# Attention on one core: probabilities and values turned by DMA as two planes of 16-bit halves instead of by TensorE

## What is computed

```python
y = einsum('bct,bcd->bdt', x, cond_weights[itok])          # (64, 64, 1024)
qkv = y @ attn_qkvw + attn_qkvb                            # 32 heads of 32, q, k and v
scores = einsum('bhqd,bhkd->bhqk', q, k) * 32 ** -0.5
probs = softmax(scores)
ctx = einsum('bhqk,bhkd->bhqd', probs, v)                  # 64 x 64 scores per sequence and head
x = x + ctx @ attn_ow + attn_ob                            # output stage
x = x + ffn(expert_lora(x))                                # expert and feed-forward stage
```

## Time and profile before

| | |
|---|---|
| median of 3 runs | 2267.62 us (2263.91 to 2267.73) |
| the profiled execution's own time | 2266.86 us |
| its span, first to last instruction | 2265.2 us |
| mean granted TensorE clock, share of full | 0.986 |
| busy: TensorE matmuls, weight loads | 2172.2 us, 1772.7 us |
| busy: VectorE, ScalarE, GpSimd | 1441.5 us, 732.3 us, 1385.6 us |

### The profile page before, as it was taken

How to read it: one execution, slowest core, us unless ns; L and a number is a source line. 1 busy time by engine, 2 the same in 40 slices (tenths; PEclk the granted TensorE clock), 3 DMA queues, 4 the chain that set the end, 5 groups by cost and what they waited for, 6 DMA issues and landing times.

```text
span 2265.2 us, 46621 instructions
## 1 busy us (share of the span) xinstructions
PE 2172.2 (96%) x18848; PEld 1772.7 (78%) x18848; DVE 1441.5 (64%) x2392; ACT 732.3 (32%) x1182; POOL 1385.6 (61%) x1135
## 2 busy tenths in 40 slices
PE   6999999999999999999999899999899999999996
PEld 5888887888877888878888678888777778777774
DVE  5344564455464454655554776566688888888986
ACT  4222242222242222332222422222344344444342
POOL 6888778877778887797776740000355555555553
PEclk9999999999999999999999999999999999999998
DMA  4112122212132112212112543557644434444432
GB/s 146 56 62 65 63 85 75 72 53 66 58 101 73 58 57 66 84 49 70 53 65 73 200 159 125 191 172 207 157 103 106 107 94 101 111 111 104 108 85 83
DMA packets 220828, 219.35 MB, mean 97 GB/s; under 512 B 83570, under 2 KB 152306, under 8 KB 220146
## 3 DMA queue, kind: packets, MB, share of 16 engines
q1 hardware_dynamic: 217794, 213.65, 31.6%
q0 software_dynamic: 2864, 3.28, 0.9%
HBM read 152.92 MB, written 50.33 MB: 90 GB/s over the span
## 4 chain that ended last, share of the span: by engine, by line
PE 83%; DVE 7%; issue 2%; POOL 2%; SPq 2%; ACT 2%; DMA 1%; POOLq 0%; DVEq 0%; ACTq 0%
PE acc L699 33%; PE acc L1543 15%; PE acc L1095 6%; PE att L1095 6%; PE att L1568 5%; PE att L730 3%; PE att L1517 3%; PE acc L1576 2%; PE att L739 2%; PE att L754 2%; DVE prob L539 2%; PE acc L1550 2%; DVE total L535 1%; PE acc L713 1%; SPq L265 1%
## 5 line engine op out<-in xcount | busy, mean ns | idle before, releaser
L699 PE MATMUL acc<-y_hi,w_slot_hi 128*128 128x512 f32 x1344 | 541.5, 403 | 26.1 <-DVE unit L556 7.5
L699 PE MATMUL acc<-y_hi,w_slot_lo 128*128 128x512 f32 x1344 | 527.1, 392 | 0.0
L699 PE MATMUL acc<-y_lo,w_slot_hi 128*128 128x512 f32 x1344 | 526.9, 392 | 0.0
L345 POOL TENSOR_TENSOR w_slot_lo<-w_raw,w_slot_hi 128x512 fp32r<-128x512 f32 x329 | 423.2, 1286 | 26.3
L699 PEld LDWEIGHTS acc<-y_hi,w_slot_hi 128*128 128x128 f32 x1344 | 254.4, 189 | 86.2 <-issue 30.3
L343 POOL CAST w_slot_hi<-w_raw 128x512 fp32r<-128x512 f32 x329 | 218.8, 665 | 155.8 <-PE acc L699 130.7
L699 PEld LDWEIGHTS acc<-y_hi,w_slot_lo 128*128 128x128 f32 x1344 | 254.3, 189 | 54.6
L699 PEld LDWEIGHTS acc<-y_lo,w_slot_hi 128*128 128x128 f32 x1344 | 254.9, 190 | 48.3
L348 POOL TENSOR_TENSOR w_raw<-w_raw 128x512 f32<-128x512 f32 x188 | 258.5, 1375 | 30.0 <-DMA w_raw<-wu 25.6
L546 DVE COPY cx<-att 128x512 f32<-128x512 f32 x63 | 43.5, 691 | 305.9 <-PE att L754 276.8
L556 DVE TENSOR_TENSOR unit<-acc,unit 128x512 f32<-128x512 f32 x144 | 98.6, 687 | 172.9 <-PE acc L699 168.3
(11 more groups left out here) (175 smaller groups left out, 3940.4 us busy)
## 6 DMA issues: line engine op xcount, KB each, us to landing
w_raw<-wu SPq DMA_DIRECT2D x192, 256.0 KB, 3.1
f_x_all<-x_T SPq DMA_DIRECT2D x64, 512.0 KB, 5.5
c_raw<-context_T SPq DMA_DIRECT2D x16, 1024.0 KB, 6.2
out<-f_raw SPq DMA_DIRECT2D x32, 512.0 KB, 3.4
context_T<-cx SPq DMA_DIRECT2D x63, 256.0 KB, 3.5
x_raw<-x SPq DMA_DIRECT2D x27, 512.0 KB, 4.5
xa<-xT SPq DMA_DIRECT2D x12, 1024.0 KB, 7.4
x_T<-xa SPq DMA_DIRECT2D x48, 256.0 KB, 2.0
```

What stands on the lines that cost most here:

```text
L345: pool.tensor_tensor(w_lo[:, k], raw, w_hi[:, k].bitcast(F32), ALU.subtract).then_inc(w_set, 1)
L699: ins = pe.matmul(bank, w[:, k, c, :], v[:, k, c, :], start=(k in (0, 1, 5) and c == 0 and i == 0), stop=(c == C // 2 - 1 and i == 2), ski ...
```

## The change

The transposes leave TensorE. ScalarE parts each fp32 word of a 128x512 plane into its upper and lower 16 bits (`words`, a copy of 1024 16-bit elements into `pw` or `vw`), issues a DMA transpose of the 128x1024 16-bit elements from its own queue (into `pv` or `vv`), and after landing joins the halves again into `prob_T` or `v_s` (another copy of 1024 elements). There are 61 x 2 such trips for the probabilities and 64 for the values; the last three iterations keep TensorE's turn (`TURNED`). Three ScalarE operations (two copies and a DMA issue) stand where one copy out of PSUM stood.

Places: scores now stand at 0, 5, 10 and 15, and in the same place TensorE mixes the iteration before. The other engines follow `behind`: VectorE normalises plane 0 one slot and plane 1 two slots behind the scores, ScalarE sends plane 0 out two slots and plane 1 three slots behind, and joins both four slots behind. Values go out at 0, 7, 10 and 15 and come back at 3, 9, 13 and 18 (in the last duo: out at 0, 2, 4, 6).

The four new tiles lie where `x_raw` lies. So a block's first three x tiles are loaded only in slots 4 and 5 of the unit before, when the trips of that place are done, and the trips that come next wait until the y products have read the tiles (`x_done`). The staging of y uses `uo[0]` from the second block on.

```diff
+    vw, vv, pw, pv = (nc.alloc_sbuf_tensor_at(n, shape, U16, offset=X_AT + 4096 + at) for n, shape, at in (
+        ("vw", [P, 2, HALF], 0), ("vv", [P, 2 * HALF // P, P], 2048),
+        ("pw", [P, 2, 2, HALF], 4096), ("pv", [P, 2, 2 * HALF // P, P], 8192)))
...
+    PLACES = (0, 5, 10, 15)
+
     def scored(U, k):
 
         duo, at = place(U, k)
-        return 4 * duo + (0, 4, 10, 15).index(at) if at in (0, 4, 10, 15) else None
-
-    def turned(U, k):
+        return 4 * duo + PLACES.index(at) if at in PLACES else None
+
...
+    def behind(U, k, steps):
+
+        q = SLOTS * U + k - steps
+        return scored(*divmod(q, SLOTS)) if q >= 0 else None
+
+    def values_out(U, k):
         duo, at = place(U, k)
-        return 4 * duo + (3, 9, 14, 19).index(at) if at in (3, 9, 14, 19) else None
-
-    def mixed(U, k):
-
+        steps = (0, 2, 4, 6) if duo == DUOS - 1 else (0, 7, 10, 15)
+        return 4 * duo + steps.index(at) if at in steps else None
+
+    def values_back(U, k):
         duo, at = place(U, k)
-        if at == 0:
...
-        return 4 * duo + (4, 10, 15).index(at) if at in (4, 10, 15) else None
-
-    def values(U, k):
-
-        duo, at = place(U, k)
-        return duo, {0: (0, 1), 3: (2, 3)}.get(at, ())
+        steps = (2, 4, 6) if duo == DUOS - 1 else (3, 9, 13, 18)
+        return 4 * duo + steps.index(at) if at in steps else None
+
+    def words(ap):
+
+        return ap.bitcast(U16).rearrange("p (n h) -> p h n", h=2)
+
+    TURNED = ITERS - 3
...
+    def stage(r):
+
+        return uo[0] if r else uo[1]
...
+            last = 16 * r - 4
+            if r and t >= 3:
                 sp.wait_ge(y_mm, i - 2)
-            elif i >= PAIRS:
-                sp.wait_ge(y_mm, i - PAIRS + 1)
-            arrived = x0_in[i // 2 - 1] if 3 <= i < PAIRS else x_in[(i - PAIRS) % 3 if i >= PAIRS else i]
+            elif r:
...
+                sp.wait_ge(y_mm, PAIRS * r)
+                if t == 0:
+                    sp.wait_ge(v_set, last + 1)
+                elif t == 1:
+                    sp.wait_ge(p_in[0], 16 * (last + 1))
+                    sp.wait_ge(p_in[1], 16 * (last + 1))
+                else:
+                    sp.wait_ge(pT_set, 2 * (last + 1))
+            arrived = x0_in[i // 2 - 1] if 3 <= i < PAIRS else x_in[t % 3]
...
             if U % UNITS == 0 and r + 1 < BLOCKS:
-                for i in range(3):
-                    load_x((r + 1) * PAIRS + i)
                 load_wc(r + 1, range(PAIRS))
             for k in range(SLOTS):
-                if mixed(*before(U, k)) is not None:
-                    store(mixed(*before(U, k)))
+                n = scored(*before(U, k))
+                if n:
+                    store(n - 1)
...
+                if U % UNITS == UNITS - 1 and r + 1 < BLOCKS:
+                    for i in {4: (0,), 5: (1, 2)}.get(k, ()):
+                        load_x((r + 1) * PAIRS + i)
...
+        def prob_out(n, p):
+            x_done(n)
+            act.wait_ge(prob_set, n * 2 + p + 1)
+            act.activation(pw[:, p], words(prob[:, p]), ACT.Copy).then_inc(pw_set, 1)
+            act.wait_ge(pw_set, n * 2 + p + 1)
+            act.dma_start_transpose(pv[:, p], pw[:, p].rearrange("p h n -> p (h n)"))\
+                .then_inc(p_in[p], 16)
+
+        def prob_back(n, p):
+            if n and p == 0:
+                act.wait_ge(c_mm, n)
+            act.wait_ge(p_in[p], 16 * (n + 1))
+            act.activation(words(prob_T[:, p]), pv[:, p].rearrange("p (h j) n -> p h (j n)", h=2), ACT.Copy)\
+                .then_inc(pT_set, 1)
+
+        def v_out(n):
+            duo, q = divmod(n, 4)
+            g, half = TURN_V[q]
+            V = 3 * duo + 1
+            x_done(n)
+            act.wait_ge(act_out, 4 * V + 4)
+            act.wait_ge(dve_out, 3 * V + 3)
+            act.activation(vw[:], words(uo[1][:, 2 * g + half]), ACT.Copy).then_inc(vw_set, 1)
+            act.wait_ge(vw_set, n + 1)
+            act.dma_start_transpose(vv[:], vw[:].rearrange("p h n -> p (h n)"))\
+                .then_inc(v_in, 16)
+
+        def v_back(n):
+            duo, q = divmod(n, 4)
             g, half = TURN_V[q]
             if duo:
-                act.wait_ge(c_mm, 4 * duo - 3 + q)
-            act.wait_ge(vt_mm, 4 * duo + q + 1)
-            act.activation(v_s[:, 4 * half:4 * half + 4, g * P:(g + 1) * P], flat(acc[:, 2 + q % 2]), ACT.Identity)\
-                .then_inc(v_set, 1)
+                act.wait_ge(c_mm, n - 3)
+            act.wait_ge(v_in, 16 * (n + 1))
+            act.activation(v_s[:, 4 * half:4 * half + 4, g * P:(g + 1) * P].bitcast(U16)
+                           .rearrange("p j (f h) -> p h j f", h=2),
+                           vv[:].rearrange("p (h j) f -> p h j f", h=2), ACT.Copy).then_inc(v_set, 1)
...
-                if scored(*last) is not None:
-                    att_exp(scored(*last))
-                if turned(U, k) is not None:
-                    att_pt(turned(U, k))
-                duo, turns = values(U, k)
-                for q in turns:
-                    turn_v(duo, q)
+                if values_back(U, k) is not None:
+                    v_back(values_back(U, k))
+                if values_out(U, k) is not None:
+                    v_out(values_out(U, k))
+                if scored(U, k) is not None:
+                    att_exp(scored(U, k))
+                for p in range(2):
+                    if (behind(U, k, 2 + p) or 0) < TURNED and behind(U, k, 2 + p) is not None:
+                        prob_out(behind(U, k, 2 + p), p)
+                if behind(U, k, 4) is not None:
+                    prob_back(behind(U, k, 4), 0)
+                    prob_back(behind(U, k, 4), 1)
...
         def att_scores(n):
-            if 0 < n < LAST:
-                dve.wait_ge(pt_mm, n * 2)
+            if n == LAST - 1:
+                dve.wait_ge(pt_mm, 2)
+            elif 0 < n < LAST:
+                dve.wait_ge(pw_set, n * 2)
...
-                if scored(*last) is not None:
-                    att_norm(scored(*last))
-                if mixed(U, k) is not None:
-                    att_ctx(mixed(U, k))
+                n = behind(U, k, 1)
+                if n is not None:
+                    att_norm(n, (0,))
+                    if n:
+                        att_ctx(n - 1)
+                if behind(U, k, 2) is not None:
+                    att_norm(behind(U, k, 2), (1,))
                 if scored(U, k) is not None:
                     att_scores(scored(U, k))
...
-        def turn_v(duo, q):
-            g, half = TURN_V[q]
-            V = 3 * duo + 1
-            if q == 2:
-                pe.wait_ge(act_out, 4 * V + 4)
-            else:
-                pe.wait_ge(dve_out, 3 * V + (3, 1, 0, 2)[q])
-            if 4 * duo + q > 1:
-                pe.wait_ge(v_set, 4 * duo + q - 1)
-            for j in range(HALF // P):
-                ins = pe.transpose(acc[:, 2 + q % 2, j * P:(j + 1) * P], uo[1][:, 2 * g + half, j * P:(j + 1) * P], ident[:])
-            ins.then_inc(vt_mm, 1)
-
...
             elif 0 < n < LAST - 1:
-                pe.wait_ge(pt_set, 2 * n)
+                pe.wait_ge(sub_set, 2 * n)
...
+            if n < TURNED:
+                pe.wait_ge(pT_set, n * 2 + 2)
+            else:
+                pe.wait_ge(pt_set, (n - TURNED) * 2 + 2)
...
         for U in range(ALL):
             block_end = U % UNITS == UNITS - 1 and U + 1 < ALL
             for k in range(SLOTS):
-                if mixed(U, k) is not None:
-                    att_ctx(mixed(U, k))
-                if turned(U, k) is not None:
-                    att_turn(turned(U, k))
-                duo, turns = values(U, k)
-                for q in turns:
-                    turn_v(duo, q)
-                if scored(U, k) is not None:
-                    att_scores(scored(U, k))
+                n = scored(U, k)
+                if n is not None:
+                    att_scores(n)
+                    if n:
+                        att_ctx(n - 1)
```

54 lines of the change are left out of this document (26 added, 28 removed).

## The result

The changed kernel takes 2335.3 us (median of 4 runs, 2333.6 to 2346.5), the kernel before 2267.7 in the same comparison: ratio 1.0305, 95% interval 1.0288 to 1.0323. It is slower by 3%; the forecast was 2223, and the range ended at 2305. The profiled execution has a span of 2332.0 us, 66.8 more than before's 2265.2.

The account below looks back on a forecast made before the run. TensorE's list was taken to bound the kernel: 6.9 us less per duo, 3.8 of stalls back, gain 3.1 times 15 = 46 us, last duo -2.2, so 2266.9 - 44 = 2223 us; range 2165 to 2305, the forecast's own 2187 to 2257.

Parts of the forecast that it names:

- What bounds, and what goes: TensorE's list bounds the kernel; it falls to 65.8 us per duo, 6.9 less, with a ceiling of 107 us.
- the waits of positions 3 and 8: TensorE's waits for VectorE at these places, 1.3 us per duo, taken to go with the spread normalisation.
- What comes: New ScalarE work per duo: ways out 2.4 us, ways back 1.0 to 1.06, 53 us of 66 in all.
- I take 1.06: Price in us of ScalarE's copy of 16-bit halves, from the bf16 quantiser's row; far end twice 1.06.
- Position 15: Probabilities joined at 52.2 us into the duo, needed by TensorE at 52.1; stall 0.1 us.
- Rival 3: Transposes land late behind weight loads, four places waiting some 5 us longer; +255 us, 2520 us; chance 0.03.
- Position 10: ScalarE's joins end at 36.3 us, mixing could begin at 34.3; TensorE stalls 2.05 us per duo.
- The break-even at 1.28 us per copy: Price of ScalarE's copy of halves at which the gain is 0; the kernel gets slower from there on.
- the forecast's slope: Stalls grow by 14 us per duo for each microsecond added to the price of ScalarE's copy of halves.
- The last duo: Ways out closer together: slot 4 waits about 1.9 us, position 5's join is 3.8 late; 3.5 - 5.7 = -2.2 us.
- Block starts: Late x tiles, up to 3 us at each of three starts, set off against up to 2.3 us back at two.
- Rival 2: Slow copies of halves make ScalarE late and the kernel slower: 2323 us at 1.5 us per copy; chance 0.20.

Follow-up runs that it names:

- loads_behind: Changed kernel, with SyncE's last two unit-weight loads at position 13 held until plane 1 of the turned probabilities has landed; 2308.5 us, ratio 1.0182.
- loads_behind_contig: Changed kernel with those two weight loads held back and joins writing contiguously (attention result zero, so only for prices); 2289.2 us, ratio 1.0099.
- joins_contiguous: Changed kernel with joins writing their halves in one contiguous piece, partings multiplied by zero (attention result zero); 2320.9 us, ratio 1.0226.
- last_duo_on_tensor: Changed kernel, with TensorE turning the last duo's values and its first iteration's probabilities; the other 15 duos keep DMA; 2330.8 us, ratio 1.0290.
- x_tiles_late: Kernel before, with a new block's first three x tiles loaded in slots 4 and 5 of the previous block's last unit; 2264.6 us, ratio 0.9982.
- cx_first: Changed kernel, with VectorE's copy of mixed values at a block's end moved ahead of the unit output and normalisation; 2335.8 us, ratio 1.0298.
- best: Kernel before with places 0, 5, 10, 15, spread normalisation and values turned by DMA for 15 duos; TensorE turns the rest; 2234.1 us, ratio 0.9850.
- issue_on_sync: Changed kernel with the DMA transposes issued by SyncE instead of ScalarE, unit-weight loads one slot later in SyncE's list; 2378.9 us, ratio 1.0484.

## Why the prediction was wrong

**What bounds, and what goes: right.** TensorE's list fell to 66.1 us a duo as worked out (65.8), and the waits of positions 3 and 8 went with the places (1.6 us; I had 1.3).

**The error in the duo** is 5.0 us (69.6 forecast, 74.55 in the duo shown): 1.7 from the stall at position 15, 1.6 from the clock, 1.0 from the stall at position 10, 0.4 from the one at position 5, 0.3 from TensorE's own work.

**What comes: three of four prices right.** Parting 1.05 (1.06), issue 1.25 (1.24), landing 3.1 (3.0) at positions 5 and 0. Wrong was "I take 1.06" for the copy of halves on the way back: 1.36. Contiguous joins take 1.6 us off a duo (loads_behind against loads_behind_contig). I had no row with a two-byte write at a four-byte step, knew it, and took one price for both ways; only the way back has the strided write, and only it is dearer.

**The step that failed most in the duo is "Position 15: joined at 52.2, needed at 52.1. Stall 0.1."** It took a landing of 3.0 us in a stretch in which SyncE issues a unit's weight loads. There it is 4.6 (4.8 in the median of all duos), and the stall 1.8. Rival 3 had landings late by 5.4 us at all four places at a price of 255 us, and I gave it 0.03. It came true in a small form, most of all at one place of four, for 27 us (loads_behind). The prediction's DMA share of 0.19 was a mean over the duo before; the share beside this transfer is 0.87.

**Position 10** was forecast at 2.05 and is 3.0 with dear joins, and 2.2 and 1.6 in the duos shown with cheap ones: in these the model of the stalls was right, as at 5 and 9, once its prices are put in. Other duos of joins_contiguous have up to 3.9 there. Left out was that TensorE's clock can fall behind such a stall: the half-speed steps cost 1.6 us in the duo shown. The forecast costed stalls by their length alone.

**The break-even at 1.28 us per copy** was therefore wrong too. Parting and joining are 1.2 on average, which by the forecast's slope still gains 1 us per duo. The duo lost 1.75, because the landing and the clock had already used up the margin.

**The last duo** was forecast at -2.2 and is -18.6. I looked for stalls in ScalarE's list and did not list what SyncE issues in the same slots: six loads of 1 MB, beside which an issue of ScalarE's took 7.1 us. Taking the last duo's transposes away gave back 10.9 us (last_duo_on_tensor). The earlier trace rows were all taken beside smaller loads; "landing at most 4.2" became 15.1.

**Block starts** were forecast at nothing, by setting late tiles against sooner weights. The sooner weights did give back what I put in (x_tiles_late, 4 us in all). But the starts cost 8 us each more. 3 to 5 of them are VectorE's order (cx_first): the copy for which the first y pair waits stands behind a unit output and a normalisation. The stretches of the third block start, changed and before, and TensorE's two new waits in the changed kernel tell most of the rest:

```profile
962.92:1016.04 53.12, 44.27 (x352) 37.41 (x350) 30.97 (x49) 28.36 (x45) 36.19 (x32) 0.90 0.42 121
...
929.21:973.55 44.34, 39.59 (x357) 34.49 (x356) 31.15 (x48) 23.77 (x44) 33.46 (x29) 0.96 0.25 78
```
```profile
976.87 0.86 PE L815 MATMUL att<-prob_T,v_s 64*32 64x64 f32 x64 [2.08 <-ACT prob_T L458]
985.26 5.21 PE L732 MATMUL att<-wc_raw,x_raw 128*128 128x128 f32 x32 [2.99 <-issue]
```

TensorE is idle for 8.9 us instead of 4.8 and busy for 4.7 us more at a lower granted clock, although its list is one turn shorter. One new wait is that of cx_first, the other is for the joined probabilities, as in every duo, and the first y pair takes 5.2 us instead of 3.7. What of the slower work belongs to which wait was not tried apart.

**The rivals.** Rival 2 named the outcome and its mechanism, ScalarE late at slot 9 and positions 5, 10 and 15, at 0.20; its condition (1.28 us per copy) was not met, its places were. Against rival 3's estimate of 10.5 us for eight blocks, from the Trainium skill's 1309 ns for 128x128 (VectorE: DVE Perf Modes, the three transpose paths), the runs show medians of 3.1 to 5.5 us, place by place, in the steady part. The Trainium skill's advice there, to turn on TensorE where the result may go to PSUM, was right here for the probabilities all the same: the kernel that leaves them on TensorE (best) is the fastest.

## What to carry to other kernels

Before a transfer is put on a path that something waits for, list what every other queue issues in those very slots: the same transpose landed in 3.1, 4.6 or 15 us in one kernel, and one wait per duo on another queue was worth 27 us. Move to DMA first what has slack of several slots (the values, best) and leave on the engine what is produced and wanted within four slots (the probabilities). And where a stall of the bounding engine is forecast, allow for its clock afterwards.

## What the hardware did that was not expected

- ScalarE, 1024 two-byte elements: reads at a four-byte step 1.046 us, writes contiguous 1.057, writes at a four-byte step 1.356. The same join of probabilities on VectorE: 0.74 to 1.84, median 1.16.
- A DMA transpose's issue holds its engine's sequencer 1.25 us, and up to 7.1 where another queue issues 1 MB loads (SyncE's own transposes in issue_on_sync: 1.23, up to 3.6).
- Landing of 128x1024 two-byte elements: 3.1 us at a DMA share of 0.35, 4.6 at 0.87, up to 15.1 at 0.99.
- TensorE worked at its lower clock level for eight steps after a stall of 3.03 us (granted clock 0.89 over the next 15 us); after one of 2.96 us in loads_behind the clock was 0.82 over 14. After stalls of 1.80 and 1.61 us it stayed at 1.00. The length alone doesn't decide: a stall of 3.34 us at 1095.76 in the changed kernel was followed by 1.00 over 15 us, one of 1.89 us at 887.85 in loads_behind_contig by 0.89. What else decides is not shown here.
